# Dense 105-word rows, PSUM operands in the second hop, and TensorE's reports behind a drain, in a graph-attention kernel

## The reference

```
e_input = sum((concat(ent[head], ent[tail]) @ fc_w.T + fc_b) * rel[etype], -1)
e       = leaky_relu(e_input, 0.2)
alpha   = exp(e - segment_max(e)[head]) / segment_sum(exp_e)[head]
agg     = segment_sum(ent[tail] * alpha, head) + ent
ent     = agg / max(norm(agg), 1e-12)          # twice
out     = layernorm(x + ent)
```

## Time and profile before

| | us |
|---|---|
| median of 3 runs | 2910.04 (2908.55 to 2920.16) |
| profiled execution, its own time | 2912.71 |
| its span, first to last instruction | 2910.3 |
| PE busy | 1099.4 (38%) |
| DVE busy | 1850.1 (64%) |
| ACT busy | 860.1 (30%) |
| POOL busy | 1780.5 (61%) |
| mean granted TensorE clock | 0.58 of full |

### The profile page before, as it was taken

How to read it: one execution, slowest core, us unless ns; L and a number is a source line. 1 busy time by engine, 2 the same in 40 slices (tenths; PEclk the granted TensorE clock), 3 DMA queues, 4 the chain that set the end, 5 groups by cost and what they waited for, 6 DMA issues and landing times. The chain is left out here.

```text
span 2910.3 us, 22387 instructions
## 1 busy us (share of the span) xinstructions
PE 1099.4 (38%) x4597; PEld 839.1 (29%) x4597; DVE 1850.1 (64%) x3677; ACT 860.1 (30%) x1608; POOL 1780.5 (61%) x1607
## 2 busy tenths in 40 slices
PE   4688602233233233223322634343433434333310
PEld 4577601122132123222212423221222322222210
DVE  6967863366556556556636567775776668577684
ACT  2334312454455455445521211110111111011121
POOL 1000057277777777777764347777677767767776
PEclk9556555555555555555555556565665656556555
DMA  3455432366676676676664562222222222222110
GB/s 89 124 152 151 137 61 65 61 117 105 117 127 98 115 130 114 103 121 121 100 105 95 69 127 84 67 79 65 79 67 64 81 63 80 65 66 62 55 56 13
DMA packets 235265, 265.66 MB, mean 91 GB/s; under 512 B 182810, under 2 KB 190123, under 8 KB 231636
## 3 DMA queue, kind: packets, MB, share of 16 engines
q1 hardware_dynamic: 184804, 205.51, 32.4%
q0 software_dynamic: 50416, 59.64, 10.3%
HBM read 141.54 MB, written 128.15 MB: 93 GB/s over the span
## 5 line engine op out<-in xcount | busy, mean ns | idle before, releaser
L574 POOL DMA_INDIRECT area<-tail,gi x784 | 805.6, 1028 | 294.1 <-issue 241.3
L574 POOL DMA_INDIRECT area<-head,gi x392 | 465.6, 1188 | 277.2 <-DVE gi L1138 145.2
L623 POOL DMA_INDIRECT out<-area,place x392 | 493.6, 1259 | 119.4 <-issue 119.4
L764 PE MATMUL psR<-area,row_t 128*98 128x512 f16 (+1 forms) x896 | 301.2, 518 | 634.8 <-DVE area L1186 216.4
L672 PE MATMUL psP<-V,vT 65*125 65x40 f32 (+1 forms) x1586 | 317.3, 388 | 170.1 <-issue 65.3
L764 PEld LDWEIGHTS psR<-area,row_t 128*98 128x98 f16 x896 | 157.5, 184 | 772.0 <-issue 535.2
L672 PEld LDWEIGHTS psP<-V,vT 65*125 65x125 f32 (+1 forms) x1586 | 310.0, 304 | 188.2 <-issue 70.2
L664 PE MATMUL psT<-ident,area 128*65 128x128 f32 x393 | 90.1, 420 | 560.5 <-issue 495.4
L664 PEld LDWEIGHTS psT<-ident,area 128*65 128x65 f32 x393 | 80.2, 229 | 569.0 <-issue 569.0
L869 ACT ACTIVATE area<-iota_h,half_hi 128x392 f16<-128x392 f16 x392 | 237.8, 607 | 9.4 <-issue 9.4
L1137 DVE COPY gi<-head_i 128x14 int32 (+1 forms) x28 | 5.0, 180 | 347.1 <-DMA rows<-area 299.4
(11 more groups left out here) (267 smaller groups left out, 2460.0 us busy)
## 6 DMA issues: line engine op xcount, KB each, us to landing
area<-rows SPq DMA_DIRECT2D x28, 1183.0 KB
tail<-area SPq DMA_DIRECT2D x50, 637.5 KB
area<-tail_digits SPq DMA_DIRECT2D x28, 896.0 KB
rows<-area SPq DMA_DIRECT2D x28, 735.0 KB
tail<-area SPq DMA_DIRECT2D x28, 595.0 KB
area<-tail SPq DMA_DIRECT2D x25, 637.5 KB
head<-area SPq DMA_DIRECT2D x25, 630.0 KB
area<-tail,gi POOLq DMA_INDIRECT x784
```

Of the source, the lines that this page charges most:

```text
L574: pool.indirect_dma_start(out=to[:, b, k, 0:tab.shape[1]], out_offset=None, in_=tab, in_offset=bass.IndirectOffsetOnAxis(ap=gi[:, b, n, k: ...
L623: pool.indirect_dma_start(out=out, out_offset=bass.IndirectOffsetOnAxis(ap=place[:, b, k:k + 1].bitcast(U32), axis=0), in_=rowO[:, b, k, 0 ...
L764: last = te.matmul(psR[g % 2][0:HH, 0:w], row_t[:, n, c, :], hot_lo[:, c, 4 * g * P:4 * g * P + w], start=c == 0 and n == 0, stop=c == HB ...
```

## The change

Tables: `head0`, `tail0`, `tail1` go; `rows0` [NPAD, 105] and `rows1` [NPAD + N, 105] hold features, a one, B and A in rows of 105 words; x of the heads goes into its own table `head_xs` through a new tile `rowX` that ACT fills. In the second hop one operand or the output of most of DVE's passes lies in PSUM (`held_...`, views of psT and psP). PE's groups are reported by `pe.drain(); pe.sem_inc(...)`. `take_rows` moves from the head of the chunk to the end of `capture` in the second hop, its sums to psM, and `choose` of group 3 to the chunk's end.

```diff
-    tail0 = dram("tail0", [N, WT])
-    head0 = dram("head0", [NPAD, WH])
-    tail1 = dram("tail1", [NPAD + N, WT])
-    rows1 = dram("rows1", [NPAD, W1])
+    rows0 = dram("rows0", [NPAD, WE])
+    rows1 = dram("rows1", [NPAD + N, WE])
+    head_xs = dram("head_xs", [NPAD, C])
...
+        flatT = psT[:, :, :].rearrange("p n x -> p (n x)")
+        held = flatT[:, 0:K * C].rearrange("p (k c) -> p k c", c=C)
+        held_A = flatT[:, 0:K * R].rearrange("p (k r) -> p k r", r=R)
+        held_typ = flatT[:, K * R:2 * K * R].rearrange("p (k r) -> p k r", r=R)
+        held_part = flatT[:, 1024 - CO - 1:1024]
+        small = flatT[:, 1024:1536]
...
+        held_ex = psP[:, 1, 512 - 2 * K:512].rearrange("p (n k) -> p n k", n=2)
+        held_decay = psP[:, :, :].rearrange("p n x -> p (n x)")[:, 0:CO * (K + 1)].rearrange("p (c k) -> p c k", k=K + 1)
...
             def store(j, b):
                 sp.wait_ge(s_nb, j + 1)
-                for to, of in ((t0, nT), (h0, nH)):
-                    for lo, hi in node_halves:
-                        sp.dma_start(to[lo:hi, cols(j, KN), :], of[lo:hi, b, :, :]).then_inc(s_nst[b], 16)
+                for lo, hi in node_halves:
+                    sp.dma_start(r0v[lo:hi, cols(j, KN), :], nR[lo:hi, b, :, :]).then_inc(s_nst[b], 16)
...
-            def head_x(j, b, i):
-                sp.wait_ge(s_gat[b], 16 * 2 * K * (i + 1))
+            def head_x(j, b):
+                sp.wait_ge(s_xc, j + 1)
                 sp.sem_inc(s_turn_sp, 1)
-                sp.dma_start(re[:, cols(j), X0:W1], rowH[:, b, :, 0:C]).then_inc(s_xc[b], 16)
+                sp.dma_start(xe[:, cols(j), :], rowX[:, b, :, :]).then_inc(s_xst[b], 16)
...
-                sp.dma_start(re[:, cols(j), 0:X0], rowO[:, b, :, 0:X0]).then_inc(s_dump[b], 16)
-                sp.dma_start(te[:, cols(j), :], rowO[:, b, :, 0:WT]).then_inc(s_dump[b], 16)
+                sp.dma_start(re[:, cols(j), :], rowO[:, b, :, :]).then_inc(s_dump[b], 16)
...
                     sp.dma_start(rowH[:, b, :, :], re[:, cols(j), :]).then_inc(s_hl[b], 16)
+                    sp.dma_start(rowX[:, b, :, :], xe[:, cols(j), :]).then_inc(s_hl[b], 16)
...
-                    gather(i * 2 + b, b, 0, head0, rowH)
-                    gather(i * 2 + b, b, 1, tail0, rowT)
+                    gather(i * 2 + b, b, 0, rows0, rowH)
+                    gather(i * 2 + b, b, 1, rows0, rowT)
...
-                    last.then_inc(tr, 1)
+                    pe.drain()
+                    pe.sem_inc(tr, 1)
...
                     te.matmul(psC, sign_lo[:, (s0 + k) % KS, :], sign_hi[:, (s0 + k) % KS, :],
-                              start=static and t0 + k == 0, stop=True, skip_group_check=True).then_inc(s_cnt, 1)
+                              start=static and t0 + k == 0, stop=True, skip_group_check=True)
+                    pe.drain()
+                    pe.sem_inc(s_cnt, 1)
...
-                for to in (nT, nH):
-                    sc_.copy(to[0:PN, b, :, 0:C], xs[0:PN, b, :, :]).then_inc(s_act, 1)
+                sc_.copy(nR[0:PN, b, :, 0:C], xs[0:PN, b, :, :]).then_inc(s_act, 1)
...
+                    if h == 0:
+                        if not static:
+                            act.wait_ge(s_xst[b], 16 * i)
+                        sc_.copy(rowX[:, b, :, :], rowH[:, b, :, 0:C]).then_inc(s_xc, 1)
...
-                link(ve.tensor_tensor(vv, agg, wide(rd[:, 0:K0], K0), ALU.mult))
-                ve.tensor_tensor(vv, vv, rowsH[:, :, 0:C], ALU.add).then_inc(s_sq, 1)
+                via, rd_, rs_, mean_ = (vv, rd, rs, mean) if h == 0 else (held[:, 0:K0, :], held_rd, held_rs, held_mean)
+                link(ve.tensor_tensor(via, agg, wide(rd_[:, 0:K0], K0), ALU.mult))
+                ve.tensor_tensor(vv, via, rowsH[:, :, 0:C], ALU.add).then_inc(s_sq, 1)
...
                     def free():
                         if ahead:
                             if h == 0:
-                                dve.wait_ge(s_xc[b], 16 * (i + 1))
+                                dve.wait_ge(s_xc, j + 1)
                             indices(j + 2, b, h)
```

More of the change, by code:

```diff
@@ L313, in build_gnn @@
         s_pr = sem("rows_projected")
-        s_xc = [sem(f"head_x_stored{b}") for b in range(2)]
-        s_seam_x = sem("seam_x_copied")
+        s_xc = sem("head_x_copied")
+        s_xst = [sem(f"head_x_stored{b}") for b in range(2)]
         s_out = sem("projections_copied")
@@ L616, in tails @@
                 pool.sem_inc(s_turn, 1)
-                gather(j, b, 1, tail1, rowT)
+                gather(j, b, 1, rows1, rowT)
             def write(j, b):
@@ L763, in look @@
                         for n in range(2):
-                            last = te.matmul(psR[g % 2][0:HH, 0:w], row_t[:, n, c, :], hot_lo[:, c, 4 * g * P:4 * g * P + w],
+                            te.matmul(psR[g % 2][0:HH, 0:w], row_t[:, n, c, :], hot_lo[:, c, 4 * g * P:4 * g * P + w],
                                              start=c == 0 and n == 0, stop=c == HB - 1 and n == 1)
-                    last.then_inc(s_look, 1)
+                    pe.drain()
+                    pe.sem_inc(s_look, 1)
                 pe.wait_ge(s_took, j * 4 + 4)
+                pe.sem_inc(s_turn_pe, 1)
+                if not (isinstance(j, int) and j < 4):
+                    pe.wait_ge(s_rank, j)
                 for k in range(K):
-                    last = te.matmul(psX[:, k:k + 1], chosen[0:HH, k * P:(k + 1) * P], ones[0:HH, 0:1], start=True, stop=True)
-                last.then_inc(s_sum, 1)
+                    te.matmul(sums[:, k:k + 1], chosen[0:HH, k * P:(k + 1) * P], ones[0:HH, 0:1], start=True, stop=True)
+                pe.drain()
+                pe.sem_inc(s_sum, 1)
             def first_hop(i, static):
@@ L1319, in chunk @@
                     H, Tl = rowH[:, b, :, :], rowT[:, b, :, :]
-                    if taking:
-                        take_rows(taking[0])
+                    if taking and h == 0:
+                        take_rows(taking[0], psX)
                     if look:
                         hots(*look)
-                    link(ve.tensor_tensor(typ[:, :, :], iota_r[:, :].unsqueeze(1).to_broadcast([P, K, R]),
+                    typ_, iota_ = (typ, iota_r) if h == 0 else (held_typ, held_iota)
+                    ex_, decay_, rd_, part_ = (ex, decay, rd, part) if h == 0 else (held_ex, held_decay, held_rd, held_part)
+                    link(ve.tensor_tensor(typ_[:, :, :], iota_[:, :].unsqueeze(1).to_broadcast([P, K, R]),
                                           wide(type_f[:, cc], K, R), ALU.is_equal))
@@ L1365, in capture @@
                             keep_A(j - 2, b)
-                        fe = first_end[:, cc]
+                        fe = (first_end if h == 0 else held_end)[:, cc]
                         link(ve.tensor_tensor(cap[:, :, :], SM[:, :, 1:K + 1], fe.unsqueeze(1).to_broadcast([P, CO + 1, K]), ALU.mult))
-                        link(ve.tensor_reduce(part[:, :], cap[:, :, :], AX.X, ALU.add))
-                        link(ve.tensor_tensor(first[:, :], first[:, :], part[:, :], ALU.add))
+                        link(ve.tensor_reduce(part_[:, :], cap[:, :, :], AX.X, ALU.add))
+                        link(ve.tensor_tensor(first[:, :], first[:, :], part_[:, :], ALU.add))
                         if nodes:
                             node_squares(j)
+                        if taking and h == 1:
+                            take_rows(taking[0], psM[:, 0:K])
                         if look:
@@ L1379, in rest @@
                         if look:
-                            choose(look[0], range(2, 4))
+                            choose(look[0], range(2, 3 if h == 1 else 4))
                     def free():
@@ L1384, in free @@
                             if h == 0:
-                                dve.wait_ge(s_xc[b], 16 * (i + 1))
+                                dve.wait_ge(s_xc, j + 1)
                             indices(j + 2, b, h)
-                    finish(h, K, b, H, r0 + j * nr, j + 1, S[:, 0:C, 1:K + 1].rearrange("p c k -> p k c"), (capture, rest), free,
+                    finish(h, K, b, H, rowX[:, b, :, :], r0 + j * nr, j + 1, S[:, 0:C, 1:K + 1].rearrange("p c k -> p k c"), (capture, rest), free,
                            static and i == 0, i)
@@ L1391, in chunk @@
                         ve.tensor_copy(place[:, b, :], write_f[:, cc]).then_inc(s_row, 1)
+                        if look:
+                            choose(look[0], range(3, 4))
                 def pair(i, static, h=h, chunk=chunk):
```

212 lines of the change are left out of this document (107 added, 105 removed).

## The result

| | us | ratio to the kernel before, 95% |
|---|---|---|
| forecast | 2595 (2530 to 2740) | |
| kernel after, first measurement | median 3066.4 (3020.67 to 3091.64, 4 runs) | 1.045 (1.031 to 1.059) |
| kernel before beside it | median 2909.3 | |
| the same file on chip 4 | median 2610.0 (2607.5 to 2614.1, 4 runs) | 0.917 (0.914 to 0.920) |
| kernel before beside it | median 2846.2 | |

The account below looks back on a forecast made before the run. POOL, issuing indirect DMAs, was taken as the engine to follow: its floor, lengthened DMAs and index waits. First hop -145, PSUM operand -125, sums -50, 5 back, less 2.7: 2595 us, range 2530 to 2740.

Parts of the forecast that it names:

- Reports behind a drain: PE's reports: an increment after a drain escapes the matmul's late report, so POOL finds first-hop indices in time; -50 us.
- the stop before chunk 4: First hop: POOL's 50.47 us gap ended at 579.45 by `gi`, traced to a late matmul report; expected to go.
- the array was free: Argument against drains waiting for late reports: in the same chunks PE took up later groups without delay.
- Sums off the head: Second hop: DVE no longer waits for sums at the chunk's start; POOL's 58 us of gaps shrink to about 8, -50.
- Rival D: Drains wait for the late report and PE stands still: second hop +218, first -67, total 3060 us; chance 0.05.
- One PSUM operand: Second hop: DVE passes with one PSUM operand stop lengthening POOL's DMAs; 136 us of excess become about 11, -125.
- First hop: Second hop starts at 1559 instead of 1704.7 us: -145, with the 47 and 50 in it; bounds -70 and -165.
- the wait for indices: First hop: x through rowX brings `gi` about 16 us earlier, ending POOL's 2.35 us wait a chunk; -47.
- The check from below: Second hop summed from 784 DMAs 991 us, seam 7.4, end 3, excess 11, gaps 8: 1020 instead of 1194.7.
- The range: Whole kernel: 2530 to 2740 us, leaving out rival D, no effect as described, nothing measurable and a little more.

Follow-up runs that it names:

- the late kernel after: Kernel after, unchanged, on a chip where TensorE's reports come late while POOL issues row transfers: 3066.4 us in the first measurement, 1.045 of the kernel before.
- the cut writes and gathers: Kernel after with 1 of 14 writes, or 1 of 14 gathers, per second-hop chunk: 2532.1 and 2533.7 us on chip 10, 2631.9 and 2623.8 on chip 8.

## Why the prediction was wrong, step by step

- **The step that failed: "Reports behind a drain".** It took for granted that an increment behind a drain is free of the late report ("If it comes at once", -50). It is not: the drain itself lasts until the report would have come. The drain in chunk 1 lasts 53.8 us on late chips, those behind the second hop's sums up to 31.6, TensorE stands still for that time, and the stop before chunk 4 stays, 38.21 us for 50.47, as POOL's timeline of the late kernel after has it:

```profile
570.42 1.76 POOL L585 DMA_INDIRECT area<-rows,gi  x1 [38.21 <-DVE gi L1157]
```

  The argument against this, that "the array was free", may well be true: the reports that come in bursts say so. But it says nothing of when a drain ends.
- **A second step: a late report beside a quicker POOL.** In "Sums off the head" PE's sums are ready at +6 us of the chunk. The kernel without any drain is 338 us slower on chip 5 than on chip 11, with reports 27 us late. The forecast asked of each removed stall what is late next, but not whether the late reports of the earlier trace rows stay.
- **Rival D was right in mechanism, and its total is partly luck.** It gave 3060 (measured 3066). Its second hop was to grow by 218 us and the first to shrink by 67; the profiles have +173.8 and -20.6, and the two errors nearly cancel. A chunk was to take 50.5 us; the second hop's 1368.5 less the seam's 7.4 is 48.6 a chunk. It shared this out as three holds of 8.8; in fact one lasts 31, or two together some 30. And the drains are the smaller part: they add 102 us on chip 5 (3044.0 - 2942.1), where the kernel without them already loses 338. Its chance of 0.05 rested on the argument about the array.
- **One PSUM operand: right in mechanism, and its sign depends on the chip.** Forecast -125, measured -151.4 (chip 11) and -155.3 (chip 10, 2766.1 against the 2610.8 of the kernel with the sums at the head). So rows 10 were read rightly, though they show one scan, and the inference of the Trainium skill ("SBUF — State Buffer", Who interferes with whom) that descriptor generation needs only the write side, by which nothing would change, disagrees: in the second hop of the kernels without drains on chip 11, which differ in DVE's operands, writes took 1172 and 989 ns. On late chips the PSUM operands cost about 200 us: 3044.0 (chip 5) and, without the first hop's drains, 3056.9 (chip 8), against 2844.5 (chip 8, one run) with SBUF operands. It fits that POOL's slower pace had covered the late reports; that is not shown.
- **Sums off the head: mis-sized.** Forecast -50, measured 0 in time. Of the waits of 11.84 us in the earlier trace rows 8.8 were the late report, and the 3 us that are left lie beside POOL. On a late chip undoing the move made it some 50 us faster (2992.8 against 3044.0). The Trainium skill's "PSUM — Partial Sum Buffer" (Engine vs sequencer instructions) advises the increment on the matmul; in time it makes no difference of over 12 us here, late it saves 102.
- **First hop: its size depends on the chip, too.** Forecast -145 to the seam's store. On chip 4 it is -73.5 (1659.8 to 1586.3), on chip 11 the parts of the change other than the PSUM operands bring 125.6, on the late chip of the first measurement -20.6. On chip 4 the wait for indices is gone, as forecast. POOL's gathers in 622 to 1476 us there, before (heads alone) and then after:

```profile
L574 POOL DMA_INDIRECT area<-head,gi x280 | 339.8, 1214 | 148.3 <-issue 86.7 <-DVE gi L1138 61.6
```
```profile
L585 POOL DMA_INDIRECT area<-rows,gi x581 | 659.9, 1136 | 194.8 <-issue 194.8
```

  The first stop of 50 us is absent from that profile of before, so there was nothing to be gained. Why the kernel before is 35 us faster on chip 4 than on chips 10 and 11 is open.
- **The check from below held.** POOL's 784 transfers, seam and gaps gave 1020 for the second hop; 1013.0 in time.
- **The range** treated chips as one. The kernel before moves by 3.5% between them (2846 to 2945), the kernel after by 17% (2610 to 3066). That 2610.0 and 2604.1 lie near the 2595 of the forecast is in part luck: the port brought 26 to 30 us more than its term, the sums 50 less, the first hop 20 to 70 less, and the kernel before is itself 29 to 64 us faster on these chips than the one that the sum started from.

What stays open: why chips differ, what holds a report, and how a hold ends. Sixteen of the 36 drains over 6 us in the second hop of the first profile after end 3.5 to 4.2 us after POOL's run; fifteen end while POOL still issues. Nor is it shown whether POOL's issuing or the traffic of its transfers makes the hold, since the cut writes and gathers took away both. A kernel with PSUM operands and a POOL slowed by other means was not tried.

## What to carry to other kernels

A report that lies far behind its matmul is not engineered away with a drain: the drain waits for it too, and stops the engine meanwhile. Assume that the lateness stays, and price every removed stall with it in the open. Whether the work or only the report is late can be read from the reports that follow: if they come faster than the engine can work, the work was done. Before believing a verdict for or against an edit on a stream that mixes TensorE with many row transfers by POOL, run it on more than one chip and compare the longest drains or reports. Where no chip may be slow, SBUF operands with dense rows (0.961 in time, 0.977 late, the latter one run) are the safer version here; with PSUM operands and no drains the kernel takes 0.903 in time and 0.996 late, and no version tried that computes everything is faster in time by more than 0.5%.

## What the hardware showed that was not expected

- On chips 5 and 8 groups of sums whose drain lasts 3.98 us in time were reported up to 27.8 us behind their recorded end, or kept a drain up to 31.8 us; on chips 4, 10 and 11 never, with the same code.
- Held reports are let go in bursts: fifteen of counting matmuls 0.03 us apart, which were handed over 0.33 us apart or slower, and two of a look-up's groups 0.1 us apart.
- A drain lasts as long as the hold: up to 53.8 us, where its usual length is 0.3 to 4.0.
- The hold shrinks with POOL's run of transfers: at most 13.5 us with its gathers alone and 8.4 with its writes alone, in runs of 18 to 19 us, against 31.6 in runs of 36.
- Granted clock was 0.554 to 0.582 in all profiles, the in-time kernel after at 0.567 and the late one at 0.555, so the clock is not what tells the chips apart.
